# Graph attention layers on one core: the first two masks are fetched in the phase before, and a new layer's first block is scored in two parts, the larger one inside the old layer

## The reference, cut to what matters

```python
def gat_conv(x, src, dst, W, a_src, a_dst, b):
    h = x @ W
    s = h @ a_src
    d = h @ a_dst
    alpha = jax.nn.leaky_relu(s[src] + d[dst], NEG_SLOPE)
    m = jax.ops.segment_max(alpha, dst, num_segments=n)
    ex = jnp.exp(alpha - m[dst])
    denom = jax.ops.segment_sum(ex, dst, num_segments=n)
    w = ex / (denom[dst] + 1e-16)
    return jax.ops.segment_sum(h[src] * w[:, None], dst, num_segments=n) + b
x = x / norms
x = gelu(gat_conv(x, src, dst, W1, as1, ad1, b1))
x = gelu(gat_conv(x, src, dst, W2, as2, ad2, b2))
x = gelu(gat_conv(x, src, dst, W3, as3, ad3, b3))
```

## Time and profile before

| | |
|---|---|
| median of 3 runs | 4100.26 us (4099.95 to 4102.75) |
| the profiled execution | 4102.09 us, of which the span of the profile is 4100.4 us |
| busy in the span | TensorE 3400.7 us (83%), VectorE 2950.7 us (72%), ScalarE 2343.8 us (57%) |
| `node_project_phase` | about 2634 to 2700 us |
| `layers_phase` | about 2701 to 3860 us |

### The profile page before, as it was taken

One profiled execution on the slowest core, in us unless ns is written; L12 is line 12 of the kernel. 1 busy time (PEld: TensorE's weight loads), 2 busy tenths in 40 slices (PEclk: granted clock), 3 DMA queues, 4 the chain that ended last, 5 costly groups with the idle time before them and its releaser, 6 DMA issues. The chain is left out here.

```text
span 4100.4 us, 67730 instructions
## 1 busy us (share of the span) xinstructions
PE 3400.7 (83%) x25575; PEld 2524.3 (62%) x25576; DVE 2950.7 (72%) x4524; ACT 2343.8 (57%) x3583; POOL 217.9 (5%) x212
## 2 busy tenths in 40 slices
PE   2656555888888888888844999689998999899799
PEld 1323234666666666666633566478887888788687
DVE  7999957999999999999944222255655664655456
ACT  2555526888888888888830111146664666444422
POOL 0000000000000000000000444200000000000010
PEclk9888877999999999999966999889999999999889
DMA  1222223111112411111143622333222322333220
GB/s 48 87 83 87 87 60 127 67 50 67 55 63 74 168 67 52 65 67 51 51 131 108 185 45 46 65 114 110 98 107 95 110 96 94 110 118 119 79 70 32
DMA packets 135860, 349.35 MB, mean 85 GB/s; under 512 B 28251, under 2 KB 106462, under 8 KB 117886
## 3 DMA queue, kind: packets, MB, share of 16 engines
q1 hardware_dynamic: 114840, 320.24, 22.2%
q0 software_dynamic: 13888, 20.07, 2.7%
q10 hardware_dynamic: 6822, 4.85, 0.4%
HBM read 279.91 MB, written 65.20 MB: 84 GB/s over the span
## 5 line engine op out<-in xcount | busy, mean ns | idle before, releaser
L890 PE MATMUL hd_psT<-ident,hd_scores 128*128 128x128 f32 (+1 forms) x5000 | 738.5, 286 | 31.7 <-ACT hd_scores L793 31.7
L802 ACT ACTIVATE hd_probsT<-hd_psT 128x768 f32<-128x768 f32 (+1 forms) x800 | 648.3, 835 | 187.8 <-PE hd_psT L890 186.7
L838 DVE SCALAR_TENSOR_TENSOR hd_scores<-hd_el,hx 128x3136 f32<-128x3136 f32 x200 | 695.8, 3479 | 24.4 <-DMA hd_mask<-mask_dram 18.4
L842 DVE CUSTOM_DVE_ANT_0 hd_scores<-hd_scores,hd_mask 128x3136 f32<-128x3136 f32 x200 | 684.1, 3420 | 8.6
L904 PE MATMUL hd_psO<-hd_probsT,hx 128*32 128x128 f32 (+1 forms) x10000 | 583.4, 286 | 100.5 <-ACT hd_probsT L802 99.7
L890 PEld LDWEIGHTS hd_psT<-ident,hd_scores 128*128 128x128 f32 (+1 forms) x5000 | 544.4, 143 | 185.6 <-issue 182.9
L793 ACT ACTIVATE hd_scores<-hd_scores,hd_negmax 128x1664 f32<-128x1664 f32 (+1 forms) x400 | 640.6, 1601 | 10.8 <-DVE hd_negmax L842 10.6
L1280 PE MATMUL ly_psO<-hx_a,ly_probsT 128*128 128x256 f32 x2500 | 585.0, 382 | 0.0
L1238 ACT ACTIVATE ly_probsT<-ly_psT 128x768 f32<-128x768 f32 (+1 forms) x300 | 249.3, 831 | 472.2 <-PE ly_psT L1269 472.2
L904 PEld LDWEIGHTS hd_psO<-hd_probsT,hx 128*32 128x32 f32 (+1 forms) x10000 | 322.8, 110 | 299.6 <-ACT hd_probsT L802 175.8
L1280 PEld LDWEIGHTS ly_psO<-hx_a,ly_probsT 128*128 128x128 f32 x2500 | 454.9, 190 | 71.5 <-issue 16.6
(11 more groups left out here) (293 smaller groups left out, 3446.6 us busy)
## 6 DMA issues: line engine op xcount, KB each, us to landing
ly_mask<-mask_dram SPq DMA_DIRECT2D x75, 1568.0 KB, 6.6
hd_mask<-mask_dram SPq DMA_DIRECT2D x50, 1568.0 KB, 6.8
mask_dram<-logc SPq DMA_DIRECT2D x200, 196.0 KB, 1.9
moe_w<-in_L_ffn_w SPq DMA_DIRECT2D x48, 512.0 KB
hd_el<-el_dram SPq DMA_DIRECT2D x5, 1568.0 KB, 10.4
hd_el<-el_slope_dram SPq DMA_DIRECT2D x4, 1568.0 KB, 13.0
x<-n_x SPq DMA_DIRECT2D x2, 3072.0 KB
n_x<-in_x SPq DMA_DIRECT2D x8, 640.0 KB, 7.3
```

The source lines that it names most:

```text
L802: nc.scalar.activation(pT[:, gi % 2, 0:w], psT[gi % 2][:, 0:w], ACT.Copy).then_inc(s_ev, 1)
L838: nc.vector.scalar_tensor_tensor(sc[:, c, :], el[:, h, 0, :], hx[:, b, o:o + 1], el[:, h, 1, :], ALU.subtract, ALU.min).then_inc(s_lk, 1)
L842: nc.vector.tensor_tensor_reduce(out=sc[:, c, :], in0=sc[:, c, :], in1=mask[:, B % 2, :], scale=1.0, scalar=3.0e38, op0=ALU.add, op1=ALU.m ...
L890: last = nc.tensor.transpose(psT[gi % 2][0:r, t * P:(t + 1) * P], sc[:, u % 3, c0:c0 + r], g["ident"][:, :])
```

## The change

There are three edits.

First, `mask` is allocated outside both phases. `node_project_phase` issues the fetches of blocks 0 and 1 on SP's queue after its own loads, and its VectorE stream waits for them as its last act. To make room, the nodes are normalized in place: `xn` is gone and L1002 writes `x`. Block 0 and 1 of `layers_phase` wait for no mask.

Second, in `layers_phase` SP issues the three loads of the bias first and then the fetches of blocks 2 to 74, each with the same wait as before.

Third, for the first block of layers 2 and 3, `first_maxima(l, part)` takes the place of `maxima`. Part 0 handles the columns of source blocks 0 to 22 (2944 columns) and stands in the last block's turn of the old layer, between `copy_el` of block 22 and `copy_x` of block 23. Part 1 handles the last 192 columns and stands where `maxima` stood. Each part leaves a minimum of its own, and one more instruction joins the two.

```diff
@@ node_project_phase
-        xn = sb("xn", [P, NB, D])
+        s_first_masks = sem("s_first_masks")
@@ SP
+            for b in range(2):
+                sp.dma_start(mask[:, b, :], g["mask_dram"][b * P:(b + 1) * P, :]).then_inc(s_first_masks, 16)
@@ VectorE
-                nc.vector.tensor_scalar(xn[:, b, :], x[:, b, :], mv[:, b, 0:1], rs[:, 1, b:b + 1],
+                nc.vector.tensor_scalar(x[:, b, :], x[:, b, :], mv[:, b, 0:1], rs[:, 1, b:b + 1],
                                         ALU.subtract, ALU.mult).then_inc(s_n, 1)
...
+            dve.wait_ge(s_first_masks, 32)
@@ layers_phase
+        EARLY = NB - 2
@@ SP
-            for B in range(BLOCKS):
-                if B >= 2:
-                    sp.wait_ge(s_nm, B - 1)
+            for l in range(LAYERS):
+                sp.dma_start(bb[:, l, :], ...).then_inc(s_bias, 16)
+            for B in range(2, BLOCKS):
+                sp.wait_ge(s_nm, B - 1)
                 b = B % NB
                 sp.dma_start(mask[:, B % 2, :], g["mask_dram"][b * P:(b + 1) * P, :]).then_inc(s_mask[B % 2], 16)
-                if B == 1:
-                    for l in range(LAYERS): ...
@@ VectorE
+            def first_maxima(l, part):
+                B, n = l * NB, 2 * (l - 1) + part
+                c = B % 3
+                cols = (slice(0, EARLY * P), slice(EARLY * P, NS))[part]
+                if part == 0:
+                    dve.wait_ge(s_mask[B % 2], 16 * (B // 2))
+                    dve.wait_ge(s_T, 4 * (B - 2))
+                dve.wait_ge(s_ec, (l - 1) * NB + (EARLY, NB)[part])
+                nc.vector.scalar_tensor_tensor(sc[:, c, cols], el[l % 2][:, 0, cols], hx[l % 2][:, 0, D:D + 1], el[l % 2][:, 1, cols],
+                                               ALU.subtract, ALU.min).then_inc(s_lkp, 1)
+                dve.wait_ge(s_lkp, n + 1)
+                nc.vector.memset(spare[:, :], 0.0)
+                nc.vector.tensor_tensor_reduce(out=sc[:, c, cols], in0=sc[:, c, cols], in1=mask[:, B % 2, cols],
+                                               scale=1.0, scalar=3.0e38, op0=ALU.add, op1=ALU.min,
+                                               accum_out=nmp[:, part:part + 1]).then_inc(s_nmp, 1)
+                if part == 1:
+                    dve.wait_ge(s_nmp, n + 1)
+                    nc.vector.tensor_tensor(nm[:, c:c + 1], nmp[:, 0:1], nmp[:, 1:2], ALU.min).then_inc(s_nm, 1)
+                    dve.wait_ge(s_nm, B + 1)
+                    nc.vector.tensor_scalar(has[:, c:c + 1], nm[:, c:c + 1], -NEG / 2, None, ALU.is_lt).then_inc(s_has, 1)
@@ VectorE, the loop over layers and blocks
-                maxima(B0)
+                if l == 0:
+                    maxima(B0)
                 maxima(B0 + 1)
...
                     if following and b >= 2:
                         copy_el(B0 + b - 2)
+                    if following and b == NB - 1:
+                        first_maxima(l + 1, 0)
                     if following and b >= 1:
                         copy_x(B0 + b - 1)
...
                     copy_el(B0 + NB - 1)
+                    first_maxima(l + 1, 1)
```

More of the change, by code:

```diff
@@ L927, in node_project_phase @@
 @phase
-def node_project_phase(nc, g, x_in, wx, hx, el, a):
+def node_project_phase(nc, g, x_in, wx, hx, el, mask, a):
     with ExitStack() as ctx:
@@ L1069, in transpose_x @@
                 for k in range(2):
-                    last = nc.tensor.transpose(psX[b % 2][:, k * P:(k + 1) * P], xn[:, b, k * P:(k + 1) * P], g["ident"][:, :])
+                    last = nc.tensor.transpose(psX[b % 2][:, k * P:(k + 1) * P], x[:, b, k * P:(k + 1) * P], g["ident"][:, :])
                 last.then_inc(s_xT, 1)
@@ L1096, in layers_phase @@
 @phase
-def layers_phase(nc, g, wx, hx, el, y_last, a):
+def layers_phase(nc, g, wx, hx, el, mask, y_last, a):
     with ExitStack() as ctx:
@@ L1102, in layers_phase @@
         sc = sb("scores", [P, 3, NS])
-        mask = sb("mask", [P, 2, NS])
         pT = sb("probsT", [P, 2, 7 * P])
@@ L1108, in layers_phase @@
         nm = sb("negmax", [P, 3])
+        nmp = sb("negmax_part", [P, 2])
         den = sb("den", [P, 3, 2])
@@ L1124, in layers_phase @@
         BLOCKS = LAYERS * NB
+        EARLY = NB - 2
         @block.sync
         def _(sp):
-            for B in range(BLOCKS):
-                if B >= 2:
-                    sp.wait_ge(s_nm, B - 1)
+            for l in range(LAYERS):
+                sp.dma_start(bb[:, l, :], a[f"L1_gnn_b{l + 1}"].rearrange("(o n) -> o n", o=1).broadcast_to([P, D])).then_inc(s_bias, 16)
+            for B in range(2, BLOCKS):
+                sp.wait_ge(s_nm, B - 1)
                 b = B % NB
                 sp.dma_start(mask[:, B % 2, :], g["mask_dram"][b * P:(b + 1) * P, :]).then_inc(s_mask[B % 2], 16)
-                if B == 1:
-                    for l in range(LAYERS):
-                        sp.dma_start(bb[:, l, :], a[f"L1_gnn_b{l + 1}"].rearrange("(o n) -> o n", o=1).broadcast_to([P, D])).then_inc(s_bias, 16)
         @block.vector
@@ L1140, in maxima @@
                 l, b, c = B // NB, B % NB, B % 3
-                dve.wait_ge(s_mask[B % 2], 16 * (B // 2) + 16)
-                if b == 0 and l:
-                    dve.wait_ge(s_ec, l * NB)
+                if B >= 2:
+                    dve.wait_ge(s_mask[B % 2], 16 * (B // 2))
                 if B >= 3:
@@ L1147, in maxima @@
                                                ALU.subtract, ALU.min).then_inc(s_lk, 1)
-                dve.wait_ge(s_lk, B + 1)
+                dve.wait_ge(s_lk, B + 1 - l)
                 nc.vector.memset(spare[:, :], 0.0)
@@ L1963, in program @@
             wx = [sbl(f"wx_{l}", [P, 2, R1]) for l in range(LAYERS)]
-            node_project_phase(nc, g, x1, wx, hxa, el[0], a)
-            layers_phase(nc, g, wx, (hxa, hxb), el, y, a)
+            mask = sbl("ly_mask", [P, 2, NS])
+            node_project_phase(nc, g, x1, wx, hxa, el[0], mask, a)
+            layers_phase(nc, g, wx, (hxa, hxb), el, mask, y, a)
         xt = sb("xt", [P, 2, NP])
```

5 lines of the change are left out of this document (3 added, 2 removed).

## The result

The changed kernel takes 4081.67 us (5 runs, 4078.45 to 4083.03) against 4100.26 us beside it: a ratio of 0.9954, with a 95% interval of 0.9942 to 0.9965. It is 18.6 us faster; the prediction said 4081.5 us and 18.8 us. The execution that was profiled took 4083.03 us, the slowest of the five.

The account below looks back on a forecast made before the run. TensorE's work plus three waits for scores at layer starts was taken to bound the layers. First masks 6.9 us plus two borders of 5.9 us give 18.8 us less than the 4100.26 median: 4081.5 us, range 4077.5 to 4085.5.

Parts of the forecast that it names:

- Three gaps bound the layers: At each layer's start TensorE waits for scores, 35.7 us in all; a microsecond off a gap is one off the end.
- First masks, 6.9 us: Start of the layers' phase: VectorE starts at 2701.22 in place of 2708.12, without waiting for the first mask; gains 6.9 us.
- Part 1, 5.9 us a border: At borders between layers, scoring only the last 192 columns takes 1.05 us in place of 6.98; gains 5.9 us each.
- Part 0, nothing: Old layer's last block: scoring 2944 columns fits VectorE's idle time before TensorE's `project` at 3098.2; costs nothing.
- The clock, nothing: At the borders TensorE's clock still falls in the shortened 3.4 us pause, so no gain is taken for it.
- The rival that the clock stays up: Clock holds over the short border pauses: 4078.9 us with one border, 4076.3 with both; chance 0.10.
- The sum: Whole kernel: 6.9 + 2 x 5.9 = 18.8 us gained, 4081.5 us against the median of 4100.26.
- The rival with the masks ahead of the weights: Projection phase's start: masks get in front of the weight loads, adding up to 10.4 us, 4091.9 us; chance 0.04.

Follow-up runs that it names:

- second profile: The changed kernel measured again without any change, beside other versions: 4082.58 us, 18.7 us less than the kernel before.
- the borders were filled: Changed kernel plus TensorE transposes of the identity in its waits at both layer borders: 4077.42 us, 5.2 us less than the changed kernel beside it.
- the kernel with the masks first: Changed kernel with the two first mask fetches issued ahead of the weights on SP's queue: 4092.85 us, 9.0 us slower than the changed kernel.
- the halves: Changed kernel with the split undone, 4094.93 us; changed kernel with the first masks fetched in the layers' phase again, 4090.63 us.

## Why the prediction was right

*Three gaps bound the layers.* Right: TensorE's waits for scores fell by 19.0 us and the time by 18.6. The pauses are 10.1, 3.3 and 3.3 us, where 10.1, 3.4 and 3.4 were forecast.

*First masks, 6.9 us.* Right: TensorE starts 7.0 us sooner after the phase's first issue (15.85 to 8.86), VectorE 0.04 us after it where 0.13 was taken. Alone it gave 7.5 us.

*Part 1, 5.9 us a border.* Right, and by the line through two widths: 1.05 us forecast and measured. The instructions take 0.42 and 0.35 us. Alone the split gave 11.8 us.

*Part 0, nothing.* Right as long as it fits: 3.29 and 3.22 us, done before TensorE's projection at both borders. What it costs without cover was mis-sized: "each microsecond past 3098.2 would be one lost per border" is too little. 4.7 us too long cost 7.8 and 8.7 us at the two borders, because the clock drops in the wait and the chain behind it runs at half speed.

*The clock, nothing.* The step said that it would fall still, and it fell in every profile of a short border. Its reason, a fall 1.1 us after the last matmul, doesn't hold in general: at the short borders of the changed kernel's two profiles the fall came from 0.7 us before the last matmul's end to 3.7 us after it. But it came back earlier in the first profile of the changed kernel, 9.2 us at 0.50 after the restarts in place of 16.4, which gave that execution 3.6 us that the sum doesn't have; in its second profile it was 13.6. The rival that the clock stays up did not come true until the borders were filled.

*The sum.* The execution that was profiled had these 3.6 us more in the layers and about 3 us less elsewhere: 1.2 ahead of the projection phase, 0.9 in it and 1.0 behind the layers. In the projection phase 0.6 of it is the clock again, 5.4 us at 0.50 after the first turned block in place of 4.1; the kernel with the masks first also normalizes in place and has 4.1 and the old length of that stretch, 35.8 us. All this is one execution, the slowest of five. The median of the whole, 18.6 and 18.7 us in two measurements, and the halves stand behind the 18.8. That 4081.5 and 4081.67 agree to 0.2 us is luck, since single runs of the changed kernel span 4.6 us.

*The rival with the masks ahead of the weights.* As a mechanism it is real, 9.0 us when the order is turned; the order in which SP issues them is what keeps it away.

## What to carry to other kernels

Where a stage can't start until the last block of the one before, compute what depends on all the other blocks inside the old stage, in the idle time of the engine that does it, and leave the smallest remainder; its price is well read from a line through two widths of the same instruction. Put such work where the trace shows the engine idle, and compare its end with the next instruction that TensorE waits for: overrunning that point cost 1.7 and 1.9 times the overrun here. Prefetches for the next phase go behind the loads that this phase waits for, and a load that isn't needed yet goes behind the one that is needed first: three small ones ahead of a mask made it come late, though here that cost no time.

## What the runs showed of the hardware

The granted clock of the same program differs from execution to execution: after its three restarts TensorE worked 3.3, 3.1 and 2.8 us at 0.50 in one profile of the changed kernel, and 5.7, 4.5 and 3.4 in another, in which the last fall came 0.4 us after TensorE had restarted. Half of the difference is time, 2.2 us here, about half of what the runs of this kernel span (4.6 us).

Transposes of the identity in the waits of a dependent chain, 34 a border, left the chain's length (5.89 us) and the pause behind it (3.31 us) as they were, and TensorE's granted clock stayed at 1.00.

Where every matmul waits for VectorE, a clock of 0.50 costs as well: `project` took 2.09 us in place of 1.14, and the chain of five such steps 8.66 in place of 6.05.
